# A reordered unit in an attention kernel: where the maximum products, the value products and two VectorE steps stand

## The chip, the core and the metric

One core of a Trainium2 chip runs the whole program. The metric is the device time of one execution in microseconds (us). Engines are named as the profile names them: PE is TensorE's matmuls and PEld its weight loads, DVE is VectorE, ACT is ScalarE, POOL is GpSimd, SP is SyncE, which here only issues DMAs.

## The reference, cut to what matters

The kernel computes a transformer block on x of shape (2, 2048, 256): attention with 16 heads of width 16, a layer norm, a small gated feed-forward part, and a second layer norm.

```
q, k, v = x @ Wq + bq, x @ Wk + bk, x @ Wv + bv      # split into 16 heads of 16
q, k    = q*cos + rot(q)*sin, k*cos + rot(k)*sin     # rotary, interleaved pairs
probs   = softmax(q @ k^T / sqrt(16))                # 2048 x 2048 for each of 2*16 heads
x1      = layernorm(x + (probs @ v))
xr, xk  = mu*x1 + (1 - mu)*previous_token(x1)        # one mu for r, one for k
x2      = sigmoid(xr @ Wr^T) * (relu(xk @ Wk^T)^2 @ Wv^T)
out     = layernorm(x1 + x2)
```

## The kernel before, in words

There are 32 heads (2 sequences x 16), and nearly all of the time is in `period(h)`, once for each. The scores of a head are 2048 x 2048. They are made twice. First, while the head before is at work, PE makes them only to find the maximum of each query row (the **maximum product**, L511, into `ring_ps`), and DVE reduces them (L1095). Then, in the head's own period, they are made again in transposed form with the negated maximum added as three more rows of the contraction (the **score**, L608, into `score_ps`), ACT takes the exponential (L783, into `probs`), and PE multiplies by the values (the **values**, L544, `pv`, into `pv_ps`). Queries and keys are each split into three bf16 parts, so a score has 96 or 99 rows of contraction; the value product is in fp32 and passes twice.

A period has 16 **units** (`kt`). One unit of PE holds

- four scores S0 to S3 of 128 x 512, each as four matmuls of 32 columns of weights side by side (one group of four);
- two maximum products m0 and m1 of the next head, 128 x 1024 each, so two groups of four each. The first is for the first half of the keys of a query tile, the second for the other;
- the values of the unit before, `pv(kt - 1)`, four matmuls in two passes.

In the kernel before they are issued in the order S0, half of m0, S1, half of m0, S2, half of m1, S3, half of m1, `pv`. Two generators make the order: `ring_ops` yields after each half of a maximum product, and the loop over j takes one half after each score.

What binds the engines to each other:

- `ring_ps` has two buffers of 1024 columns. m(k) may start when DVE has reduced m(k-2) (`ring_freed`).
- `score_ps` has three banks. Score n may start when exponential n-3 is done (`exps_done`). `probs` has two buffers of one unit, so ACT's unit kt waits for `pv(kt - 2)` (`pv_done`).
- `period_ops(h)` lists what DVE does in each unit, in order: the two reductions; `cut` (L1074, the 16 row maxima of the whole next head, negated) behind the last reduction of that head, which falls in unit 12; `turn` (L1105, a transpose of `pv_ps` once the head before is summed up) in unit 0; `recip` (L1110, 1/sum) in unit 1; and for heads 17 to 24 `stat` in unit 8 (layer norm statistics, L1121 and L1124), for heads 24 to 27 `flip` in units 6 and 10.
- The maxima of head h+1 go from DVE's `cut` to POOL, which splits them into three bf16 parts with four small operations in a row (`cut_maxima`, L890 to L896), and then to PE, which turns them with two small matmuls (**negatives**, L524, waits on `neg_cut`) at the start of unit 14 (`NEG_CYCLE`). ACT copies the result, SP stores it with a DMA, and the next period starts when it has landed. PE takes its instructions in the order in which they are issued, so whatever is behind the negatives waits with them.
- PE waits for `turn` (`pv_turned`) before the first values of a head, in unit 1.
- POOL's loop, one pass for each head: `lay_v` (the values of a later head), `add_context` (context x 1/sum, added to x; waits for `recip`), a quarter of the rotary work of a coming group of four heads (`turn_quad`, `cut_quad_high`, `_mid`, `_low`), and last `cut_maxima`.
- In the last head there are no maximum products; its units already hold S0, S1, S2, `pv`, S3.

Of the kernel before, what the change touches and what calls it, by code (L numbers as in the profile page):

```python
# [21 lines left out]
BLOCKS = SEQ // TOK  # L22
# [3 lines left out]
LAST = ALL_HEADS - 1  # L26
# [27 lines left out]
R_PER_CYCLE = 1  # L54
FLIPS = 4 * 4
POOL_BLOCKS = 2
STAT_HEAD, STAT_CYCLE = HEADS + 1, 8
FLIP_HEAD, FLIP_CYCLES = HEADS + 8, (6, 10)
MIXED_BUFS = 3
# [24 lines left out]
def period_ops(h):  # L84

    for kt in range(TILES):
        ops = []
        for u in (2 * kt + EARLY, 2 * kt + EARLY + 1):
            if u < MAX_UNITS:
                if h + 1 <= LAST:  # L90
                    ops.append(("max", h + 1, u))
                    if u == MAX_UNITS - 1:
                        ops.append(("cut", h + 1, 0))
            elif h + 2 <= LAST:
                ops.append(("max", h + 2, u - MAX_UNITS))
        if 0 < h < LAST and kt < 2:
            ops.append((("turn", "recip")[kt], h - 1, 0))
        if kt == STAT_CYCLE and 0 <= h - STAT_HEAD < POOL_BLOCKS * TPB:
            ops.append(("stat", h - STAT_HEAD, 0))
        flip = (h - FLIP_HEAD) * len(FLIP_CYCLES)  # L100
        if kt in FLIP_CYCLES and 0 <= flip < POOL_BLOCKS * TPB:
            ops.append(("flip", flip + FLIP_CYCLES.index(kt), 0))
        yield ops
# [7 lines left out]
def ring_len(ops):  # L111
    return sum(kind in ("max", "neg") for kind, _, _ in ops)
# [9 lines left out]
def item(h, kt, j):  # L122

    return h * UNITS + kt * BLOCKS + j + h + (kt >= NEG_CYCLE and h < LAST)


def neg_item(h):

    return item(h - 1, NEG_CYCLE, 0) - 1
# [7 lines left out]
def build(nc, x_tok, x_ch, w_qk, b_qk, w_v, b_v, w_rkv, mu, cos_t, sin_t, ident, ident_h, out):  # L137
# [3 lines left out]
    with ExitStack() as ctx:  # L141
        def sb(name, shape, dt=F32):
            return ctx.enter_context(nc.sbuf_tensor(name, shape, dt))
# [34 lines left out]
        recip = sb("recip", [P, CTX_BUFS, TILES])  # L178
# [157 lines left out]
        def _(sp):  # L336
# [83 lines left out]
            def land(n):  # L420

                sp.wait_ge(flip_ready, (n + 1) * TPB)
                after(sp, edge_ready, n if n > 1 else 0)
                src = flipped_y[:, n % 2, :].rearrange("p (m b t) -> p b m t", m=CHUNKS * TPB, t=VCOLS)
                dst = y_ch[:, n % 2].rearrange("p c (q a t) -> p a (c q) t", q=TPB, t=VCOLS)
                for a in range(P // VCOLS):
                    for b in range(P // VCOLS):
                        sp.dma_start(dst[b * VCOLS:(b + 1) * VCOLS, a], src[a * VCOLS:(a + 1) * VCOLS, b])\  # L428
                            .then_inc(y_landed[n], DMA)

            for h in range(LAST):
# [9 lines left out]
                block, odd = divmod((h + 1 - FLIP_HEAD) * len(FLIP_CYCLES), TPB)  # L441
                if not odd and 1 <= block <= POOL_BLOCKS:
                    land(block - 1)
            for n in range(POOL_BLOCKS, BLOCKS):
                land(n)
# [16 lines left out]
        def _(pe):  # L462
# [55 lines left out]
            def negatives(h, bank):  # L518

                pe.wait_ge(neg_cut, h + 1)  # L520
                rows = neg_cuts[:, :, :].rearrange("p a t -> p (a t)")
                for g in range(0, PARTS * TILES, VCOLS):
                    top = min(g + VCOLS, PARTS * TILES)
                    mm = pe.matmul(bank[g:top, 0:P], rows[:, g:top], id16[:, :], start=True, stop=True)  # L524
                return mm

            def ring_ops(ops, k):

                for kind, h, unit in ops:
                    if kind == "max":  # L530
                        yield from maximum(k, h, unit)
                        k += 1
                    elif kind == "neg":
                        pe.wait_ge(ring_freed, k + 1)
                        negatives(h, ring_ps[k % 2]).then_inc(ring_filled, 1)
                        k += 1
                        yield
# [40 lines left out]
            def beside(kt):  # L578

                if kt == 1:  # L580
                    pe.wait_ge(ring_freed, RING_CREDIT + RING_TOTAL)
                if kt > 0:
                    for _ in itertools.islice(first_r, R_PER_CYCLE):
                        pass
# [4 lines left out]
            def period(h):  # L589

                k = RING_BASE[h]

                pe.wait_ge(neg_in[h % STACKS], (h // STACKS + 1) * DMA)
                for kt, ops in enumerate(period_ops(h)):

                    work = ring_ops(ops, k)
                    k += ring_len(ops)
                    if kt == NEG_CYCLE and h < LAST:
                        n = neg_item(h + 1)
                        pe.wait_ge(exps_done, n + 1)  # L600
                        negatives(h + 1, score_ps[n % SCORE_BANKS]).then_inc(scores_ready, 1)
                    for j in range(BLOCKS):
                        n = item(h, kt, j)
                        queries = q_stack[0:ROWS_M, h % STACKS, :].rearrange("r (c j t) -> r j c t", j=BLOCKS, t=VCOLS)

                        pe.wait_ge(exps_done, n + 1)
                        for g in range(0, P, VCOLS):
                            mm = pe.matmul(score_ps[n % SCORE_BANKS][g:g + VCOLS, :],  # L608
                                           k_stack[0:ROWS_M, h % STACKS, kt * P + g:kt * P + g + VCOLS],
                                           queries[:, j],  # L610
                                           start=True, stop=True)
                        mm.then_inc(scores_ready, 1)
                        next(work, None)
                        if h == LAST and j == BLOCKS - 2:
                            pv_before(h, kt)
                    for _ in work:
                        pass
                    if h < LAST:
                        pv_before(h, kt)
                    else:  # L620
                        beside(kt)
                if h == LAST:
                    for _ in first_r:
                        pass

            def pv_before(h, kt):

                if kt > 0:
                    if kt == 1:
                        pe.wait_ge(v_aug_ready, h + 1)  # L630
                        after(pe, pv_turned, h)
                    pv(h, kt - 1)
                elif h > 0:
                    pv(h - 1, TILES - 1)
# [232 lines left out]
        def _(pool):  # L867
# [31 lines left out]
            def add_context(h):  # L899

                pool.wait_ge(recip_ready, h + 1)
                after(pool, z_ready, h)
                pool.tensor_tensor(ctx_part[:, :, :], ctx_turn[:, h % CTX_BUFS, :, 0:HEAD_DIM],  # L903
                                   recip[:, h % CTX_BUFS].unsqueeze(2).broadcast_to([P, TILES, HEAD_DIM]), ALU.mult)\
                    .then_inc(ctx_ready, 1)
                pool.wait_ge(ctx_ready, h + 1)
                z = z_heads[:, :, h, :]
                pool.tensor_tensor(z, z, ctx_part[:, :, :], ALU.add).then_inc(z_ready, 1)
# [26 lines left out]
            def cut_quad_low(g):  # L935

                pool.wait_ge(quad_step, g * QUAD_STEPS)
                pool.tensor_tensor(cuts[:, g % 2, 2, :], raw, cuts[:, g % 2, 1, :], ALU.subtract).then_inc(quad_ready, 1)  # L938
# [35 lines left out]

            for h in range(ALL_HEADS - 2):
                lay_v(h + 2)
                add_context(h)
                g = 2 + h // QUAD
                if g < QUADS:
                    if h % QUAD == 0:  # L980
                        turn_quad(g)
                    if h % QUAD == 1:
                        cut_quad_high(g)
                    if h % QUAD == 2:
                        cut_quad_mid(g)
                    if h % QUAD == 3:
                        cut_quad_low(g)
                for n in range(POOL_BLOCKS):
                    if h == STAT_HEAD + (n + 1) * TPB - 1:
                        inverse(rstd, n * TPB, (n + 1) * TPB, (n + 1) * TPB, rstd_ready)  # L990
                        normalise(n)
                cut_maxima(h + 2)


            add_context(LAST - 1)
            for n in range(POOL_BLOCKS, BLOCKS):
                inverse(rstd, n * TPB, (n + 1) * TPB, (n + 1) * TPB, rstd_ready)
# [331 lines left out]
```

## Time and profile before

| | |
|---|---|
| median of 3 runs | 1533.99 us (1533.17 to 1534.14) |
| the profiled execution | 1533.71 us, its span 1531.9 us |
| granted TensorE clock, mean | 0.999 |
| PE busy | 1515.3 us, 99% |
| DVE busy | 1339.2 us, 87% |
| ACT busy | 1147.2 us, 75% |
| POOL busy | 335.0 us, 22% |
| DMA | 69.35 MB, mean 45 GB/s |

Busy times are those of the records. Matmuls overlap each other in them, and a reduction or an exponential starts a little before the one ahead of it has ended, so the start of one to the start of the next tells more than the mean duration.

### The profile page before, as it was taken

The page shows a single profiled execution, that of the slowest core. Times are in us where ns is not written, and L with a number is a line of the kernel's source. Part 1 is how long each engine was busy: PE and PEld are TensorE (multiplying, and loading weights), DVE is VectorE, ACT ScalarE, POOL GpSimd, SP SyncE. Part 2 cuts the span into 40 slices and gives each one's busy share as a digit, 9 for nine tenths or more (in the row PEclk, how much of TensorE's full clock was granted, in tenths as well). Part 3 has the DMA queues.
Part 4 walks back from the last instruction along what each step waited for, and adds up shares of the span by engine and source line. Part 5 has one row for each costly group of instructions (what it writes and reads, how often), then busy time and mean ns, then how long its engine had stood idle before and what let it go on. Part 6 is the DMA issues. An engine that isn't in the chain of part 4 may idle for free.

```text
span 1531.9 us, 49389 instructions
## 1 busy us (share of the span) xinstructions
PE 1515.3 (99%) x22016; PEld 728.9 (48%) x22016; DVE 1339.2 (87%) x1413; ACT 1147.2 (75%) x2212; POOL 335.0 (22%) x346
## 2 busy tenths in 40 slices
PE   8999999999999999999999999999999999999998
PEld 3344444444444445444444444454444444443476
DVE  5568999999999999999999999999999999998586
ACT  3338777787787787877877878778777787778855
POOL 2510322132211222132213221042212000000145
PEclk9999999999999999999999999999999999999999
DMA  7724111121112110121112111200111212000102
GB/s 231 239 92 143 29 23 23 23 78 23 23 23 78 23 18 10 22 76 23 23 23 78 23 23 23 75 15 13 23 23 23 37 23 37 2 3 2 29 29 83
DMA packets 48389, 69.35 MB, mean 45 GB/s; under 512 B 23920, under 2 KB 33904, under 8 KB 46384
## 3 DMA queue, kind: packets, MB, share of 16 engines
q1 hardware_dynamic: 45936, 62.81, 17.7%
q8 instruction: 173, 2.83, 0.8%
q10 hardware_dynamic: 2240, 3.38, 0.6%
q14 instruction: 40, 0.33, 0.1%
HBM read 26.97 MB, written 11.53 MB: 25 GB/s over the span
## 4 chain that ended last, share of the span: by engine, by line
PE 93%; DVE 2%; SPq 1%; DMA 1%; POOL 1%; ACT 1%; issue 1%; POOLq 0%; ACTq 0%
PE ring_ps L511 29%; PE score_ps L608 28%; PE pv_ps L544 28%; PE score_ps L488 2%; SPq L428 1%; PE ring_ps L570 1%; PE pv_ps L488 1%; PE score_ps L498 1%; PE score_ps L682 1%; DMA xz<-x_ch 1%; DVE tile_max L1095 0%; PE score_ps L666 0%; PE ring_ps L498 0%; PE pv_ps L666 0%; DVE stats L1121 0%
## 5 line engine op out<-in xcount | busy, mean ns | idle before, releaser
L1095 DVE TENSOR_REDUCE tile_max<-ring_ps 128x1 f32<-128x1024 f32 x1024 | 1204.3, 1216 | 138.5 <-PE ring_ps L511 136.6
L783 ACT ACTIVATE probs<-score_ps 128x512 f32<-128x512 f32 x2048 | 1057.6, 602 | 257.9 <-PE score_ps L608 255.8
L608 PE MATMUL score_ps<-q_stack,k_stack 99*32 99x512 bf16 x8192 | 830.6, 380 | 1.3 <-ACT probs L783 0.9
L511 PE MATMUL ring_ps<-k_stack,q_stack 96*32 96x512 bf16 x8192 | 828.6, 380 | 0.5 <-DVE tile_max L1095 0.4
L544 PE MATMUL pv_ps<-probs,v_aug 128*32 128x512 f32 x4096 | 538.5, 592 | 0.0
L608 PEld LDWEIGHTS score_ps<-q_stack,k_stack 99*32 99x32 bf16 x8192 | 250.7, 95 | 313.9 <-ACT probs L783 146.5
L511 PEld LDWEIGHTS ring_ps<-k_stack,q_stack 96*32 96x32 bf16 x8192 | 249.3, 96 | 302.0 <-DVE tile_max L1095 109.8
L544 PEld LDWEIGHTS pv_ps<-probs,v_aug 128*32 128x32 f32 x4096 | 142.3, 111 | 86.4
L890 POOL TENSOR_TENSOR neg_cuts<-neg_max,zeros 128x16 bf16<-128x16 f32 x32 | 7.1, 222 | 711.0 <-DVE neg_max L1074 711.0
L883 POOL TENSOR_TENSOR v_aug<-v_all,b_v_s 128x256 f32<-128x256 f32 x32 | 23.4, 732 | 278.3 <-PE pv_ps L544 255.9
L488 PE MATMUL score_ps<-xz,w_qk_s 128*32 128x512 f32 x384 | 47.7, 618 | 5.5 <-DMA w_qk_s<-w_qk 4.4
L903 POOL TENSOR_TENSOR ctx_part<-ctx_turn,recip 128x256 f32<-128x256 f32 x32 | 20.0, 624 | 123.7 <-DVE recip L1110 123.7
L743 ACT ACTIVATE probs<-score_ps,b_qk_s 128x512 f32<-128x512 f32 x21 | 14.4, 688 | 30.5 <-PE score_ps L488 30.5
L913 POOL TENSOR_TENSOR rope<-rope 128x2048 f32<-128x2048 f32 x7 | 32.1, 4580 | 22.1 <-DMA rope<-qk_raw 22.1
L570 PE MATMUL ring_ps<-w_rkv_s,rope 128*32 128x256 f32 (+1 forms) x224 | 31.3, 379 | 1.4 <-ACT q_stack L814 1.4
L914 POOL TENSOR_TENSOR rope<-rope 128x2048 f32<-128x2048 f32 x7 | 32.1, 4581 | 0.0
L920 POOL TENSOR_TENSOR rope<-rope 128x2048 f32<-128x2048 f32 x7 | 32.0, 4571 | 0.1
L1173 DVE SCALAR_TENSOR_TENSOR rope<-rope,mu_s 128x512 f32<-128x512 f32 x32 | 21.9, 747 | 9.1 <-ACT rope L808 8.9
L931 POOL TENSOR_TENSOR rope<-rope 128x2048 f32<-128x2048 f32 x7 | 28.8, 4114 | 0.1
L938 POOL TENSOR_TENSOR rope<-rope 128x2048 bf16<-128x2048 f32 x7 | 28.8, 4111 | 0.1
L827 ACT ACTIVATE v_all<-score_ps 128x512 f32<-128x512 f32 x14 | 7.6, 597 | 25.8 <-PE score_ps L682 25.8
L570 PEld LDWEIGHTS ring_ps<-w_rkv_s,rope 128*32 128x32 f32 (+1 forms) x224 | 21.7, 144 | 10.3 <-issue 6.4
(99 smaller groups left out, 529.7 us busy)
## 6 DMA issues: line engine op xcount, KB each, us to landing
qk_raw<-probs SPq DMA_DIRECT2D x28, 256.0 KB, 4.0
rope<-qk_raw SPq DMA_DIRECT2D x7, 1024.0 KB, 4.8
rope<-qk_raw SPq DMA_DIRECT2D x14, 512.0 KB, 6.8
q_stack<-rope SPq DMA_DIRECT2D x31, 192.0 KB, 3.6
k_stack<-rope SPq DMA_DIRECT2D x31, 192.0 KB, 4.2
xz<-x_tok SPq DMA_DIRECT2D x2, 2048.0 KB, 12.5
q_stack<-rope SPq DMA_DIRECT2D x31, 128.0 KB, 3.7
k_stack<-rope SPq DMA_DIRECT2D x31, 128.0 KB, 3.7
```

The lines of the kernel that those rows point to most:

```text
L488: mm = pe.matmul(bank[r:r + VCOLS, :], w_qk_s[:, c, m + r:m + r + VCOLS], x_s[:, b, c, t:t + TOK], start=c == 0, stop=c == CHUNKS - 1)
L511: mm = pe.matmul(ring_ps[k % 2][g:g + VCOLS, c * TOK:(c + 1) * TOK], q_stack[0:ROWS, buf, qt * P + g:qt * P + g + VCOLS], k_stack[0:ROWS, ...
L544: mm = pe.matmul(pv_ps[j * VCOLS:(j + 1) * VCOLS, :], v_aug[:, h % 2, kt, :], probs[:, kt % 2, j, :], start=kt == 0, stop=kt == TILES - 1, ...
L570: mm = pe.matmul(r_ps[n][g:g + width, q * DIM:(q + 1) * DIM], mixed[:, n % MIXED_BUFS, 0, c, q * P + g:q * P + g + width], w_rkv_s[:, 0, c ...
L608: mm = pe.matmul(score_ps[n % SCORE_BANKS][g:g + VCOLS, :], k_stack[0:ROWS_M, h % STACKS, kt * P + g:kt * P + g + VCOLS], queries[:, j], s ...
L783: act.activation(probs[:, kt % 2, j, :], score_ps[n % SCORE_BANKS][:, :], ACT.Exp, scale=SCALE).then_inc(exps_done, 1)
L913: pool.tensor_tensor(raw, raw, cos_s, ALU.mult).then_inc(quad_step, 1)
L914: pool.tensor_tensor(swapped, swapped, sin_s, ALU.mult).then_inc(quad_step, 1)
L920: pool.tensor_tensor(raw, raw, swapped, ALU.add).then_inc(quad_step, 1)
L931: pool.tensor_tensor(raw, raw, cuts[:, g % 2, 0, :], ALU.subtract).then_inc(quad_step, 1)
L938: pool.tensor_tensor(cuts[:, g % 2, 2, :], raw, cuts[:, g % 2, 1, :], ALU.subtract).then_inc(quad_ready, 1)
L1095: dve.reduce_max(tile_max[:, h % 2, unit // 2, unit % 2:unit % 2 + 1], slot[:, :], AX.X)\
```

## The change

It moves instructions and neither adds nor removes any.

1. PE, heads 0 to 30: a unit is now S0, S1, the whole of m0, S2, `pv(kt - 1)`, S3, the whole of m1. (The last head keeps its order.)
2. DVE: `turn` stands between the two reductions of unit 0 and no longer behind both.
3. DVE: `recip` stands behind the reductions of unit 4 and no longer of unit 1.
4. POOL: `add_context(h)` stands behind the quarter of rotary work and no longer ahead of it.

```diff
+RECIP_CYCLE = 4
@@ period_ops
-        if 0 < h < LAST and kt < 2:
-            ops.append((("turn", "recip")[kt], h - 1, 0))
+        if 0 < h < LAST and kt == 0:
+            ops.insert(1, ("turn", h - 1, 0))
+        if 0 < h < LAST and kt == RECIP_CYCLE:
+            ops.append(("recip", h - 1, 0))
@@ tensor engine, period, loop over j
                         mm.then_inc(scores_ready, 1)
-                        next(work, None)
-                        if h == LAST and j == BLOCKS - 2:
+                        if j == 1:
+                            for _ in range(2):
+                                next(work, None)
+                        if j == BLOCKS - 2:
                             pv_before(h, kt)
                     for _ in work:
                         pass
-                    if h < LAST:
-                        pv_before(h, kt)
-                    else:
+                    if h == LAST:
                         beside(kt)
@@ gpsimd, loop over heads
                 lay_v(h + 2)
-                add_context(h)
                 g = 2 + h // QUAD
                 ...
+                add_context(h)
```

PE before, around the negatives (L524), in the order in which it issues. L608 are scores, L511 halves of maximum products, L544 the values; "x4" is one group.

```order
L608 MATMUL score_ps<-q_stack,k_stack 32x512 x4
L511 MATMUL ring_ps<-k_stack,q_stack 32x512 x4
L544 MATMUL pv_ps<-probs,v_aug 32x512 x4
L524 MATMUL score_ps<-id,neg_cuts 32x128
L524 MATMUL score_ps<-id,neg_cuts 16x128
L608 MATMUL score_ps<-q_stack,k_stack 32x512 x4
L511 MATMUL ring_ps<-k_stack,q_stack 32x512 x4
```

The values were the last thing in a unit and stood just ahead of the negatives. The same place now; the lines of the file are three further down (L611, L514, L547, L527).

```order
L611 MATMUL score_ps<-q_stack,k_stack 32x512 x8
L514 MATMUL ring_ps<-k_stack,q_stack 32x512 x8
L611 MATMUL score_ps<-q_stack,k_stack 32x512 x4
L547 MATMUL pv_ps<-probs,v_aug 32x512 x4
L611 MATMUL score_ps<-q_stack,k_stack 32x512 x4
L514 MATMUL ring_ps<-k_stack,q_stack 32x512 x8
L527 MATMUL score_ps<-id,neg_cuts 32x128
L527 MATMUL score_ps<-id,neg_cuts 16x128
L611 MATMUL score_ps<-q_stack,k_stack 32x512 x8
L514 MATMUL ring_ps<-k_stack,q_stack 32x512 x8
```

The second maximum product is now the last thing in a unit, and the values stand between the third score and the fourth.

DVE before, from one head's cut (L1074) to the next's: L1095 are the reductions, L1105 is `turn`, L1110 `recip`.

```order
L1074 TENSOR_REDUCE neg_max<-tile_max 128x16
L1095 TENSOR_REDUCE tile_max<-ring_ps 128x1 x8
L1105 STREAM_TRANSPOSE ctx_turn<-pv_ps 128x512
L1095 TENSOR_REDUCE tile_max<-ring_ps 128x1 x2
L1110 RECIPROCAL recip<-ctx_turn 128x16
L1095 TENSOR_REDUCE tile_max<-ring_ps 128x1 x22
L1074 TENSOR_REDUCE neg_max<-tile_max 128x16
```

And now, for the same stretch:

```order
L1077 TENSOR_REDUCE neg_max<-tile_max 128x16
L1098 TENSOR_REDUCE tile_max<-ring_ps 128x1 x7
L1108 STREAM_TRANSPOSE ctx_turn<-pv_ps 128x512
L1098 TENSOR_REDUCE tile_max<-ring_ps 128x1 x9
L1113 RECIPROCAL recip<-ctx_turn 128x16
L1098 TENSOR_REDUCE tile_max<-ring_ps 128x1 x16
L1077 TENSOR_REDUCE neg_max<-tile_max 128x16
```

The transpose is one reduction earlier, the reciprocal six later, and the cut still follows the 32nd reduction of a head.

## Rows read from the trace of the kernel before

**Rows 1.** The page, part 1: busy time and share of each engine.
```profile
PE 1515.3 (99%) x22016; PEld 728.9 (48%) x22016; DVE 1339.2 (87%) x1413; ACT 1147.2 (75%) x2212; POOL 335.0 (22%) x346
```

**Rows 2.** The page, part 5: busy, mean ns of one, idle before it and releaser.
```profile
L1095 DVE TENSOR_REDUCE tile_max<-ring_ps 128x1 f32<-128x1024 f32 x1024 | 1204.3, 1216 | 138.5 <-PE ring_ps L511 136.6
L608 PE MATMUL score_ps<-q_stack,k_stack 99*32 99x512 bf16 x8192 | 830.6, 380 | 1.3 <-ACT probs L783 0.9
L511 PE MATMUL ring_ps<-k_stack,q_stack 96*32 96x512 bf16 x8192 | 828.6, 380 | 0.5 <-DVE tile_max L1095 0.4
```

**Rows 3.** The waits: who waited for whom, us in total, times, longest.
```profile
PEld score_ps L608 <- ACT probs L783: 146.5, 619, 0.8
PEld ring_ps L511 <- DVE tile_max L1095: 109.8, 335, 0.6
```

**Rows 4.** Timeline, head 8, PE: start us, length, what, merged.
```profile
448.37 1.09 PE L544 MATMUL pv_ps<-probs,v_aug 128*32 128x512 f32 x8
...
450.44 0.40 PE L511 MATMUL ring_ps<-k_stack,q_stack 96*32 96x512 bf16 x4
...
451.10 1.03 PE L544 MATMUL pv_ps<-probs,v_aug 128*32 128x512 f32 x8
...
464.13 1.03 PE L544 MATMUL pv_ps<-probs,v_aug 128*32 128x512 f32 x8
...
476.98 0.39 PE L511 MATMUL ring_ps<-k_stack,q_stack 96*32 96x512 bf16 x4
477.19 1.04 PE L544 MATMUL pv_ps<-probs,v_aug 128*32 128x512 f32 x8
...
479.80 1.04 PE L544 MATMUL pv_ps<-probs,v_aug 128*32 128x512 f32 x8
...
480.68 0.22 PE L524 MATMUL score_ps<-id,neg_cuts 128*16 128x128 bf16 x2
...
480.88 0.45 PE L511 MATMUL ring_ps<-k_stack,q_stack 96*32 96x512 bf16 x4
```

**Rows 5.** Timeline, head 8, DVE; in brackets the idle time before.
```profile
445.17 2.36 DVE L1095 TENSOR_REDUCE tile_max<-ring_ps 128x1 f32<-128x1024 f32 x2 [0.25 <-PE ring_ps L511]
447.44 0.71 DVE L1105 STREAM_TRANSPOSE ctx_turn<-pv_ps 128x512 f32<-128x512 f32 x1
448.07 2.32 DVE L1095 TENSOR_REDUCE tile_max<-ring_ps 128x1 f32<-128x1024 f32 x2
450.31 0.23 DVE L1110 RECIPROCAL recip<-ctx_turn 128x16 f32<-128x16 f32 x1
...
453.06 2.36 DVE L1095 TENSOR_REDUCE tile_max<-ring_ps 128x1 f32<-128x1024 f32 x2 [0.31 <-PE ring_ps L511]
...
476.55 2.36 DVE L1095 TENSOR_REDUCE tile_max<-ring_ps 128x1 f32<-128x1024 f32 x2 [0.26 <-PE ring_ps L511]
478.94 0.19 DVE L1074 TENSOR_REDUCE neg_max<-tile_max 128x16 f32<-128x32 f32 x1
```

**Rows 6.** Timeline, head 8, POOL, units 12 and 13.
```profile
479.21 0.22 POOL L890 TENSOR_TENSOR neg_cuts<-neg_max,zeros 128x16 bf16<-128x16 f32 x1 [23.08 <-DVE neg_max L1074]
...
480.11 0.22 POOL L896 TENSOR_TENSOR neg_cuts<-neg_rest,neg_cuts 128x16 bf16<-128x16 f32 x1
```

**Rows 7.** Timeline, head 8, PE's weight loads ahead of unit 14.
```profile
480.44 0.12 PEld L524 LDWEIGHTS score_ps<-id,neg_cuts 128*32 128x32 bf16 x2 [0.51 <-ACT probs L783]
```

**Rows 8.** Timeline, head 17, DVE, unit 8.
```profile
845.55 0.42 DVE L1121 BATCH_NORM_STATS2 stats<-xz 128x6 f32<-128x256 f32 x1
...
846.10 4.77 DVE L1095 TENSOR_REDUCE tile_max<-ring_ps 128x1 f32<-128x1024 f32 x4
```

**Rows 9.** Timeline, head 8, ACT, unit 13.
```profile
478.57 2.07 ACT L783 ACTIVATE probs<-score_ps 128x512 f32<-128x512 f32 x4 [0.55 <-PE score_ps L608]
```

**Rows 10.** Timeline, the opening, PE: a whole maximum product, then fp32 projections.
```profile
76.68 0.62 PE L511 MATMUL ring_ps<-k_stack,q_stack 96*32 96x512 bf16 x8
77.12 1.90 PE L488 MATMUL score_ps<-xz,w_qk_s 128*32 128x512 f32 x16
```

## The prediction

> **What bounds the kernel now.** I read the page's busy times first: PE 99% of the span, DVE 87%, ACT 75%, POOL 22% [rows 1]. Then the groups by line: scores and maximum products have almost no PE idle time ahead of them (1.3 and 0.5 us in all) [rows 2]. Then the waits: weight loads wait 146.5 us for exponentials and 109.8 us for reductions [rows 3], but a load stands ahead of its matmul, so most of that is hidden. Last the timeline of one ordinary head, number 8, to see what a unit costs and where it is longer.
>
> From the values of unit 1 to those of unit 6 PE takes (464.13 - 451.10) / 5 = 2.606 us a unit [rows 4]. One group of four has 0.218 us, the values the rest, 2.606 - 8 x 0.218 = 0.86. That is PE streaming without a gap, and the change leaves its amount alone. Units 6 to 11 take (477.19 - 464.13) / 5 = 2.612. One unit a head is much longer: 451.10 - 448.37 = 2.73 [rows 4]. So all that any order can win is the excess over 2.606: 0.12 a head there, and 0.006 in each later unit. What it can lose is any wait that becomes longer than the lead of PE's loads.
>
> Times below are within a unit, in us, with 0 at the first score. New places on PE: S0 0, S1 0.22, m0 0.44 and 0.65, S2 0.87, values 1.09 to 1.95, S3 1.95, m1 2.17 and 2.39, end 2.606. Before: m0 0.22 and 0.65, m1 1.09 and 1.53, values 1.74.
>
> **Durations used.** From the start of a maximum product's last group to its reduction, where DVE was idle: that group of unit 2 begins at 451.10 + 0.86 + 3 x 0.218 = 452.61, the reduction at 453.06, so 0.45 [rows 4, 5]. From one reduction to the next (447.44 - 445.17) / 2 = 1.135; a reduction lasts 1.216 [rows 2, 5]. From its end to the matmul that waited for its buffer: 448.07 + 2.32 = 450.39 to 450.44, 0.05 [rows 4, 5].
>
> **The excess at the head's start goes.** Before, the transpose (448.07 - 447.44 = 0.63 until the next reduction) stood behind both reductions of unit 0, so those of unit 1 were late, and m1 of unit 2 had to wait: the load that began at 450.44 [rows 4, 5]. Now m0 of unit 0 is reduced from 1.37 (behind m1 of the unit before, filled at 2.39 + 0.45 = 0.23 of this one). The transpose follows at 2.50; the values it needs are done at 1.09 + 1.09 = 2.18. The reduction of m1, ready at 2.84, starts at 3.13 and frees its buffer at 4.40, wanted at 4.78. That of m0 in unit 1 starts at 4.27 and frees at 5.54, wanted at 5.65. No wait is left, with 0.11 to spare. Gain 0.124 x 30 heads = 3.7 us; bounds 0 (the 0.11 is used up) and 3.7. PE waits for the transpose ahead of the values of unit 1, at 3.70; it ends at 3.21.
>
> **The negatives become late.** This is the term that decides. The chain is: last reduction of a head in unit 12, cut, four POOL operations, PE's load for the negatives, due at the start of unit 14. Head 8: the second reduction of the pair at 476.55 starts at 476.55 + 1.135 = 477.69, the cut at 478.94, POOL at 479.21, its last operation ends at 480.11 + 0.22 = 480.33, and PE's load begins 0.11 later, at 480.44 [rows 5, 6, 7]. So 2.75 from reduction to load. The matmul runs at 480.68 [rows 4]: the load, which had waited for POOL, came only 0.24 ahead of it. There is no more slack than that.
> Before, the product was filled at 476.98 + 0.45 = 477.43 and its reduction queued 0.26 behind that of m0. Now m1 is the last thing in unit 12: its last group begins 2.606 + 0.218 = 2.82 ahead of unit 14, is filled 2.37 ahead of it, and DVE is idle then (m0's reduction makes room at 2.50, m1 comes at 2.84). The load comes 2.75 - 2.37 = 0.38 behind the place where PE could have started the negatives. With 0.02 from load to matmul and the loads of the next score, 0.40 of standstill. Everything is queued behind the negatives on PE: S0 of unit 14 and all that follows. 30 heads x 0.40 = +12.0 us. Lower bound 0.28 (the weight load's own 0.12 [rows 7] turns out to be hidden): 8.4. Upper bound 0.38 + 0.12 + 0.12 for loads not hidden: 0.62, 18.6. I take 0.40, since the wait at 450.44 shows a matmul starting right behind what freed it.
> Head 30 apart: no maximum products follow unit 12, so PE is not full there. The standstill is 0.4 too, but the values of unit 11 (0.86) are already done when m1 ends. I take -0.5, bounds -1 and +1.
>
> **The exponentials.** The fourth one used to be far ahead of need and is not now. The first starts 0.52 behind S0 (478.57 against 477.19 + 0.86 = 478.05), and four take 2.07 [rows 4, 9]. S3 at 1.95 is taken up at 2.47 and done at 3.07 + 0.05, which is 0.52 in the next unit. S2 (0.87) and the values (1.09) need it: hidden, 0.35 spare. In unit 14 the negatives take one of the three score banks, and there S1 needs it, at 0.22. That would be a standstill of 0.30 of its own; it is covered by the 0.40 ahead of it, and is the price if the chain through POOL were quicker than I think.
>
> **Statistics, heads 17 to 24.** 846.10 - 845.55 = 0.55 on DVE behind m1 of unit 8 [rows 8]. The next m0 is then reduced from 2.84 + 1.135 + 0.55 = 4.52 and frees at 5.79, wanted at 5.65: 0.14 x 8 = +1.1 us. Before, it delayed m0 by little, since that was queued anyway. The flips (heads 24 to 27) stand at the same place; I count 0 for them, at most the same 1.1.
>
> **Reciprocal and context.** In unit 4 the reciprocal (0.23 [rows 5]) shifts m0's reduction to 4.20 at most, freed at 5.47, wanted at 5.65: hidden. Who waits for it is POOL's context, which now stands behind at most two rotary operations; POOL is busy 22% [rows 1] and had waited 23.08 us idle for the cut in head 8 [rows 6]. Nothing on PE waits for the context before the tail. 0.
>
> **The small excess.** S3's loads have more lead now (the second exponential is under way by 1.2, so the first is done, and S3 is at 1.95), and m1's too. Of 0.006 x 10 units x 30 heads = 1.8 us I take half, -0.9; bounds -1.8 and, since the cause is not visible, +1.8.
>
> **Sum.** 12.0 + 1.1 - 3.7 - 0.5 - 0.9 = +8.0 on the profiled execution's 1533.7 (span 1531.9, 1.8 outside it): 1541.7. The median of the runs shown is 0.3 higher; I leave the forecast at 1541.7.
>
> **Rivals.**
> A. The order wins and nothing is late. It needs a chain from reduction to load shorter by 0.4, and the fourth exponential earlier too. Then 1533.7 - 3.7 - 0.9 - 0.5 + 1.1 = 1529.7. For it: the excess at the head's start is plain in the timeline. Against it: the load for the negatives already waited for POOL, and the move of m1 is arithmetic of PE's order. The point from which it decides: both below 0.05 a head.
> B. The chain is partly hidden and the fourth exponential binds, 0.30 x 30 = 9.0: 1533.7 + 9.0 + 1.1 - 5.1 = 1538.7.
> C. The standstill is longer than the arithmetic, 0.6: S1 also waits, or loads are exposed. 18.0 + 1.1 - 5.1 = +14.0: 1547.7.
> D. Two groups of one kind in a row stream faster than alternating ones, so a unit's floor falls. The opening has whole maximum products in a row: 77.12 - 76.68 = 0.44 for two groups, 0.22 each [rows 10], not less than 0.218. If three pairs a unit saved 0.005 each, 496 units would give 7.4 and the time would be 1534.3, no change.
> The Trainium skill bears on D: "TensorE: Matmul & The Clock Gate", section Back-to-back issue gap, gives a gap of N / 2.4 ns plus about 2.5, which is 216 ns for 512 columns; if the eight groups of a unit fell to that from 0.218, the estimate by that page is 0.016 a unit, 8 us in all. The trace has no run of bf16 groups at that gap.
>
> **Chances.** Forecast 0.64, B 0.12, C 0.13, A 0.07, D 0.04. A measurement tells 0.2% (3.1 us) from no change. Slower: forecast, B and C, less a little for B's lower end, 0.87. Same: D and that end, 0.06. Faster: A, 0.07. The range runs from B's lower half to most of the way to C: 1537.0 to 1546.0.
>
> **What would show it.** Right: PE idle ahead of the negatives' line, about 0.4 x 31, put down to POOL; the load for them right behind POOL's last operation; the unit after a head's first values back at 2.61; a longer unit behind the statistics in heads 17 to 24; the reduction of unit 12's m1 starting some 2.4 ahead of unit 14 and not 3.0. Wrong: heads no longer than before (16 x 2.606 + 0.12 + 0.06 = 41.9 us), or standstills that fall in every unit.

## The result: 0.36% slower, by a late chain that gives up more than the order wins

| | median | against before, 95% interval |
|---|---|---|
| before, measured again beside it | 1533.84 us (6 runs) | |
| changed | 1539.55 us (1539.03 to 1540.32, 6 runs) | 1.0036 [1.0026, 1.0046] |
| forecast | 1541.7, range 1537.0 to 1546.0 | 1.0051 |

All times here and below are medians of fast runs; one slow run of the kernel before, 3252.78 us beside e1 to e4, is left out.

The profiled execution has a span of 1537.2 us, 5.3 more than before. Part 1 of its page, to be held against [rows 1]:

```profile
PE 1512.5 (98%) x22016; PEld 768.9 (50%) x22016; DVE 1344.2 (87%) x1413; ACT 1199.9 (78%) x2212; POOL 335.0 (22%) x346
```

PE's busy time fell by 2.8 us while the program became longer: PE now stands still somewhere. Yet the waits of its weight loads, to be held against [rows 3], are nearly gone for scores and maximum products. PE itself now has idle time ahead of the negatives (who waited for whom: us in all, times, longest):

```profile
PEld score_ps L611 <- ACT probs L786: 18.4, 53, 0.6
PEld score_ps L527 <- ACT probs L786: 15.5, 20, 2.0
PEld ring_ps L514 <- DVE tile_max L1098: 12.2, 48, 0.5
PE score_ps L527 <- ACT probs L786: 7.2, 30, 0.3
PE score_ps L527 <- POOL neg_cuts L899: 1.4, 1, 1.4
```

109.8 us of waiting for reductions became 12.2, and 146.5 for exponentials 18.4. (The idle time of the same loads that is put down to issue, where nothing in the profile holds them, rose from 66.2 and 54.2 to 164.2 and 138.6.) None of that was worth much: PE had had only 1.3 and 0.5 us of idle time there [rows 2]. What counts are the last two lines, PE's own idle time ahead of the negatives: 8.6 us in 31 heads, where the kernel before had 0.3 us, once. Even that is only a part, as the next rows show. (The loads for the negatives, L527, don't show it as clearly: they had waited 16.4 us before, and now 15.5 put down to ACT and 7.7 put down to issue.) The same head as in [rows 4, 5], PE's timeline at the start of unit 14 (start us, length, what):

```profile
480.39 1.06 PE L547 MATMUL pv_ps<-probs,v_aug 128*32 128x512 f32 x8
481.25 0.41 PE L611 MATMUL score_ps<-q_stack,k_stack 99*32 99x512 bf16 x4
481.47 0.63 PE L514 MATMUL ring_ps<-k_stack,q_stack 96*32 96x512 bf16 x8
482.33 0.23 PE L527 MATMUL score_ps<-id,neg_cuts 128*32 128x128 bf16 x2 [0.24 <-ACT probs L786]
```

Two groups from 481.47 end their turn at 481.47 + 0.43 = 481.90, and the negatives run at 482.33: 0.43 of standstill. The bracket shows only 0.24 of it, since the records of the matmuls before it run on, and names ACT. Its exponentials say otherwise:

```profile
479.12 2.29 ACT L786 ACTIVATE probs<-score_ps 128x512 f32<-128x512 f32 x4 [0.31 <-PE score_ps L611]
481.72 0.60 ACT L786 ACTIVATE probs<-score_ps 128x512 f32<-128x512 f32 x1 [0.31 <-PE score_ps L611]
```

The negatives take the bank of three scores back, the second of unit 13, and its exponential is the third of the four that end at 481.41. The one behind them, for the fourth score, ends at 482.32, when the load for the negatives has already begun (482.30), so nothing of ACT held it. DVE, POOL and PE's loads show who did:

```profile
479.56 1.22 DVE L1098 TENSOR_REDUCE tile_max<-ring_ps 128x1 f32<-128x1024 f32 x1 [0.24 <-PE ring_ps L514]
480.81 0.19 DVE L1077 TENSOR_REDUCE neg_max<-tile_max 128x16 f32<-128x32 f32 x1
```

```profile
481.08 0.22 POOL L893 TENSOR_TENSOR neg_cuts<-neg_max,zeros 128x16 bf16<-128x16 f32 x1 [19.41 <-DVE neg_max L1077]
...
481.97 0.22 POOL L899 TENSOR_TENSOR neg_cuts<-neg_rest,neg_cuts 128x16 bf16<-128x16 f32 x1
```

```profile
482.30 0.12 PEld L527 LDWEIGHTS score_ps<-id,neg_cuts 128*32 128x32 bf16 x2 [0.70 <-issue]
```

POOL ends at 482.19 and the load begins 0.11 later, the same step as in [rows 6, 7]; the whole chain takes 482.30 - 479.56 = 2.74, as before. Only its start has moved: 2.34 ahead of the negatives' due time (481.90) and no longer 2.97 (477.69 to 479.80 + 0.86 = 480.66).

The head's start went as forecast. DVE there, to be held against [rows 5]:

```profile
445.78 2.36 DVE L1098 TENSOR_REDUCE tile_max<-ring_ps 128x1 f32<-128x1024 f32 x2 [0.24 <-PE ring_ps L514]
448.05 0.71 DVE L1108 STREAM_TRANSPOSE ctx_turn<-pv_ps 128x512 f32<-128x512 f32 x1
448.68 4.65 DVE L1098 TENSOR_REDUCE tile_max<-ring_ps 128x1 f32<-128x1024 f32 x4
```

The transpose now takes up idle time that DVE had between the reductions of two units, and four reductions follow without a gap until DVE has caught up. PE's unit 2 is as short as its neighbours.

From the starts of the values in every unit of heads 0 to 29, summed by kind, changed less before:

| | before, a unit | after, a unit | units | sum, us | forecast |
|---|---|---|---|---|---|
| unit 2 of a head | 2.734 | 2.602 | 29 | -3.8 | -3.7 |
| the unit with the negatives | 2.617 | 3.054 | 30 | +13.1 | +12.0 |
| behind the statistics | 2.618 | 2.776 | 8 | +1.3 | +1.1 |
| all others | 2.612 | 2.599 | 413 | -5.1 | -0.9 |
| head 30 and after, net of the first start | | | | +0.3 | -0.5 |

That is +5.8 at the last values, and +5.7 in the medians. In the last row, the starts from head 30 on give +1.0, but the very first values of the program start 0.7 earlier. The values stand 0.65 earlier in a unit now, and in the last head they don't, so 0.7 of the +1.0 is that shift of place and no time lost.

### The profile page after: what moved, and what is told of

It reads as the page before. It is cut to its first block, busy times and chain, and to the rows that moved or that the text cites. A ratio compares the mean times of both kernels' runs of the same rounds, so it can differ in the third digit from the quotient of the medians.

```text
span 1537.2 us, 49389 instructions
## 1 busy us (share of the span) xinstructions
PE 1512.5 (98%) x22016; PEld 768.9 (50%) x22016; DVE 1344.2 (87%) x1413; ACT 1199.9 (78%) x2212; POOL 335.0 (22%) x346
## 4 chain that ended last, share of the span: by engine, by line
PE 92%; DVE 2%; ACT 2%; SPq 1%; DMA 1%; POOL 1%; issue 1%; POOLq 0%; ACTq 0%
PE score_ps L611 28%; PE ring_ps L514 28%; PE pv_ps L547 28%; PE score_ps L491 2%; ACT probs L786 1%; SPq L431 1%; PE ring_ps L573 1%; PE pv_ps L491 1%; PE score_ps L501 1%; PE score_ps L685 1%; DMA xz<-x_ch 1%; PE score_ps L527 0%; PE pv_ps L669 0%; PE ring_ps L501 0%; PE score_ps L669 0%
## 5 line engine op out<-in xcount | busy, mean ns | idle before, releaser
L786 ACT ACTIVATE probs<-score_ps 128x512 f32<-128x512 f32 x2048 | 1110.2, 598 | 211.2 <-PE score_ps L611 155.5
L611 PE MATMUL score_ps<-q_stack,k_stack 99*32 99x512 bf16 x8192 | 744.2, 380 | 1.0 <-ACT probs L786 0.7
L514 PE MATMUL ring_ps<-k_stack,q_stack 96*32 96x512 bf16 x8192 | 645.0, 379 | 0.2 <-DVE tile_max L1098 0.2
L547 PE MATMUL pv_ps<-probs,v_aug 128*32 128x512 f32 x4096 | 540.8, 592 | 0.0
L514 PEld LDWEIGHTS ring_ps<-k_stack,q_stack 96*32 96x32 bf16 x8192 | 265.7, 97 | 297.6 <-issue 164.2
L611 PEld LDWEIGHTS score_ps<-q_stack,k_stack 99*32 99x32 bf16 x8192 | 260.8, 95 | 283.6 <-issue 138.6
L547 PEld LDWEIGHTS pv_ps<-probs,v_aug 128*32 128x32 f32 x4096 | 148.1, 111 | 80.0
```

The lines of the kernel that those rows point to most:

```text
L514: mm = pe.matmul(ring_ps[k % 2][g:g + VCOLS, c * TOK:(c + 1) * TOK], q_stack[0:ROWS, buf, qt * P + g:qt * P + g + VCOLS], k_stack[0:ROWS, ...
L547: mm = pe.matmul(pv_ps[j * VCOLS:(j + 1) * VCOLS, :], v_aug[:, h % 2, kt, :], probs[:, kt % 2, j, :], start=kt == 0, stop=kt == TILES - 1, ...
L611: mm = pe.matmul(score_ps[n % SCORE_BANKS][g:g + VCOLS, :], k_stack[0:ROWS_M, h % STACKS, kt * P + g:kt * P + g + VCOLS], queries[:, j], s ...
L786: act.activation(probs[:, kt % 2, j, :], score_ps[n % SCORE_BANKS][:, :], ACT.Exp, scale=SCALE).then_inc(exps_done, 1)
```

## The experiments

Each was timed with the kernel before beside it on the same chip: e1 to e4 on one chip (before 1534.06), e5 to e7 on a second (1534.38), e8 and e9 on a third (1534.30). Ratios are to that one, with 95% intervals. Where a time is compared in us with the changed kernel's 1539.55, that was taken in another sitting, and half a microsecond can't be told.

**e1, the maxima a unit earlier.** The cut then falls in unit 11, and the negatives stay.

```diff
-EARLY = 2 * LEAD
+EARLY = 2 * LEAD + 2
```

> The changed kernel, with every maximum product one unit earlier (EARLY 8 instead of 6), so the cut falls in unit 11 and the negatives, still at the start of unit 14, find their chain done 2.6 us earlier. The theory (PE stands still for 0.446 us a head because the chain reduction, cut, four POOL operations ends late, 12.9 us over 29 heads): that wait goes. By its second part the score S1 of unit 14 then waits for the fourth exponential of unit 13, 0.30 a head by the prediction's arithmetic, so only 0.15 x 30 = 4.4 us come back: 1535. Rival 1, that the chain was all of it and the exponential is in time: 0.446 x 30 = 13.4 us come back, 1526. Rival 2, that the standstill has another cause (the turn of the negatives itself, the score bank): no change, 1539.5, and PE's load for the negatives still waits.

Measured: 1532.72 us, 0.9989 of before [0.998, 0.9999]. The unit with the negatives is 2.839, 0.24 over the others, where it had been 0.45. POOL, PE and PE's loads there:

```profile
437.62 0.22 POOL L899 TENSOR_TENSOR neg_cuts<-neg_rest,neg_cuts 128x16 bf16<-128x16 f32 x1
```

```profile
439.74 0.61 PE L514 MATMUL ring_ps<-k_stack,q_stack 96*32 96x512 bf16 x8
440.17 0.23 PE L527 MATMUL score_ps<-id,neg_cuts 128*16 128x128 bf16 x2
```

```profile
439.96 0.10 PEld L527 LDWEIGHTS score_ps<-id,neg_cuts 128*16 128x16 bf16 x2
439.97 0.31 PEld L611 LDWEIGHTS score_ps<-q_stack,k_stack 99*32 99x32 bf16 x4
440.61 0.10 PEld L611 LDWEIGHTS score_ps<-q_stack,k_stack 99*32 99x32 bf16 x4 [0.34 <-ACT probs L786]
```

```profile
439.96 0.60 ACT L786 ACTIVATE probs<-score_ps 128x512 f32<-128x512 f32 x1 [0.31 <-PE score_ps L611]
```

POOL is done 2.3 us ahead, and the negatives follow the maximum product 0.43 after its start, without a gap. The standstill is one score later, at the load of S1 at 440.61, and this time ACT is the right name: the fourth exponential ends at 439.96 + 0.60 = 440.56, 0.05 ahead of that load. Both rivals fail: the time is neither 1526 nor 1539.5, and the load for the negatives no longer waits. The second wait had been hidden behind the first, at 0.24 a head and not the 0.30 of the arithmetic. The gain of 6.8 us over the changed kernel is more than the 4.4 expected.

**e2, the same with the negatives in unit 13, between the values and S3.**

```diff
-NEG_CYCLE = TILES - LEAD + 1
+NEG_CYCLE = TILES - LEAD
 def item(h, kt, j):
-    return ... + (kt >= NEG_CYCLE and h < LAST)
+    return ... + ((kt, j) >= (NEG_CYCLE, BLOCKS - 1) and h < LAST)
 # PE and ACT: negatives and copy_neg ahead of j == BLOCKS - 1
```

> As e1, and the negatives stand in unit 13 between the values and S3 instead of at the start of unit 14; ACT copies them between its third and fourth exponential. The chain ends 0.4 us into unit 13, the negatives are issued at 1.95, and S3 behind them needs only the second exponential (done at 1.7). The theory: no standstill of either kind, 13.4 us less than the changed kernel: 1526, some 8 us below the kernel before. Rival: an order of this kind has a standstill wherever the negatives take a bank, then it is at the level of e1 (1535).

Measured: 1528.29 us, 0.9962 [0.9947, 0.9977]. The unit with the negatives is 2.606 on average, 0.006 over an ordinary one, so both waits are gone. It is 2 us short of the forecast: an ordinary unit is 2.600 and not 2.597, and unit 2 has 0.04 again (0.06 in e6). Why unit 2 has it wasn't settled.

**e3, PE's order alone.** Transpose, reciprocal and context where they were before.

```diff
-RECIP_CYCLE = 4
+RECIP_CYCLE = 1
-            ops.insert(1, ("turn", h - 1, 0))
+            ops.append(("turn", h - 1, 0))
 # and add_context(h) ahead of the rotary work again
```

> The changed kernel with PE's new order alone: the transpose behind both reductions of unit 0, the reciprocal in unit 1, and POOL's context ahead of the rotary work, as before the change. The theory: m1 is ready at 2.84 in a unit now, so the transpose starts at 3.97 and ends at 4.68, while the values of unit 1 want it at 3.70: PE stands still about 1.0 us a head, 30 us in all: 1570. Rival: the transpose's place only moves the wait for the ring (0.22 a head): 1546. If the move of the transpose was worth only the 3.7 us that the excess had cost before: 1543.

Measured: 1572.87 us, 1.0251 [1.0236, 1.0266]. DVE and PE in units 0 and 1 of head 8:

```profile
457.12 0.70 DVE L1108 STREAM_TRANSPOSE ctx_turn<-pv_ps 128x512 f32<-128x512 f32 x1
```

```profile
454.20 1.07 PE L547 MATMUL pv_ps<-probs,v_aug 128*32 128x512 f32 x8
...
457.93 0.64 PE L547 MATMUL pv_ps<-probs,v_aug 128*32 128x512 f32 x4 [0.92 <-issue]
```

The values of unit 1 start 0.11 behind the transpose's end (457.82), 3.73 after the last ones and not 2.60: 1.13 a head. e8 below has the reciprocal and the context in their old places too, but the transpose in its new one, and takes 1539.07. So it is the transpose's place that counts, and in the new order it is worth not 3.7 us but 33.

**e4, the first maximum product in alternating halves again.**

```diff
-                        if j == 1:
-                            for _ in range(2):
-                                next(work, None)
+                        if j < 2:
+                            next(work, None)
```

> The changed kernel with the first maximum product in halves between the scores again (S0, half, S1, half, S2, values, S3, m1 whole). Tests where the shorter unit comes from (2.597 us in the changed kernel, 2.606 to 2.612 before). Theory: a change of kind behind two groups of one kind costs 215 ns from start to start and any other step 219; this order has one such step a unit (m1 to S0) instead of three, so 2.605 in an undisturbed unit, 0.008 x 496 = 4 us more. On top, m0 wants its buffer at 0.22 instead of 0.44: by the arithmetic 0.1 a head in unit 2 and 0.36 in the eight statistics heads, 6 us. Sum: 1549. Rival: the shorter unit comes from the values' new place and the longer lead of the loads, then the undisturbed unit stays at 2.597 here and the time is about 1545.

Measured: 1548.24 us, 1.009 [1.0074, 1.0107]. The median unit is 2.605 against 2.599, near the theory of the step. Of the 8.7 us over the changed kernel that is only some 2.5. The rest is m0 waiting for its buffer: unit 2 has 2.712 (3.2 us in all), the units behind the statistics 2.956 (1.4), and those behind the flips 2.761 (1.3, which nobody had forecast; in the changed kernel the flips cost nothing, 2.597). The starts of the groups, medians in ns from one to the next over some 460 units, beginning with the values' two passes:

```
before   V 432 V 428 S 219 m 218 S 219 m 219 S 219 m 219 S 219 m 219 V   2611
changed  V 432 V 428 S 219 m 219 m 215 S 219 S 215 m 219 m 215 S 219 V   2600
e4       V 432 V 428 S 219 m 218 m 215 S 219 m 218 S 219 m 218 S 219 V   2605
e5       V 432 V 428 S 218 S 215 m 219 m 215 S 224 S 227 m 220 m 215 V   2613
e9       V 432 V 428 S 219 S 215 m 219 m 215 S 219 m 219 S 219 m 219 V   2604
```

It is not the second of a pair that comes sooner. It is what stands behind the pair, 215 and not 219. "A change of kind behind a pair" says too much, though: the opening of the kernel before has one place with four groups of maximum products in a row, and they start 220, 215 and 215 ns apart, with the next kind 216 behind the last. In the timeline:

```profile
96.09 1.05 PE L511 MATMUL ring_ps<-k_stack,q_stack 96*32 96x512 bf16 x16
96.95 1.92 PE L498 MATMUL pv_ps<-w_v_s,xz 128*32 128x256 f32 x32
```

Those four groups take 0.866 in all. So the plainer reading is that each change of kind costs about 4 ns, once, from the start of the first group of the new kind to the next start: nine changes in a unit before, six now, eight in e4, seven in e9, five in e5. The values fit (432 for their first pass, 428 for the second). Groups of one kind in a row also use the same columns of weights here, so kind and weights aren't told apart.

**e5, all in pairs.** As e2, with the values behind the second score.

```diff
-                        if j == BLOCKS - 2:
+                        if j == (BLOCKS - 3 if h < LAST else BLOCKS - 2):
                             pv_before(h, kt)
```

> As e2 (maxima a unit earlier, negatives in unit 13 behind the values), with the values between the second score and the third: S0, S1, m0 whole, values, S2, S3, m1 whole, so that scores come in pairs too. Theory of the step (215 ns for a change of kind behind two groups of one kind, 219 else): four such steps a unit instead of three, 2.596 instead of 2.600, 2 us less in all. But the values now want the fourth exponential of the unit before at 0.87, and by the durations it is done at 0.81 at the earliest, as the fourth score comes when the third is still waited for: at best hidden, else up to 0.1 a unit. So between 1526 (step theory, all hidden) and 1575 (0.1 in every unit). Rival: the step depends on something else and the unit is 2.600 with the wait apart.

Measured: 1535.36 us, 1.0007 [0.9998, 1.0016]. The row above has three of the four steps of 215; the fourth, from the second score to the maximum product, is 227, and the one ahead of it 224. In these two PE waits a few ns. Loads of scores now wait for ACT 1476 times, 478.7 us in all, where the changed kernel had 53 such waits. In one unit of the timeline the exponential that started at 460.98 ends at 461.58, and the load for the second score, which takes its bank, begins at 461.63. So it is the second score that waits, for the exponential three scores back, and not the values for the fourth, as the expectation had it. A unit is 2.613, 17 ns over the 2.596 of the theory, while the order was to win 4.

**e6, the statistics between the reductions too.** As e2, and

```diff
-            ops.append(("stat", h - STAT_HEAD, 0))
+            ops.insert(1, ("stat", h - STAT_HEAD, 0))
```

> As e2, with the layer norm statistics of heads 17 to 24 between the two reductions of unit 8 instead of behind both. Theory: DVE is idle for about 0.34 us there in every unit, so of the 0.21 a head by which unit 9 was longer in e2 nothing is left: 8 x 0.21 = 1.7 us less than e2 (1528.3), 1526.6. Rival: the statistics cost the same wherever they stand, 1528.3.

Measured: 1526.78 us (1526.57 to 1526.94), 0.9951 [0.9939, 0.9964]. The eight units behind the statistics have 2.601 on average, after 2.808 in e2. The times alone hardly part e6 from e2 (the intervals overlap); these units do. It is the fastest version found, 7.6 us below the kernel before and 12.8 below the changed one.

**e7, the chain made longer.** The changed kernel with one more POOL operation ahead of the last.

```diff
+                pool.tensor_tensor(neg_spare[:, :], neg_rest[:, :], zeros[:, :], ALU.add).then_inc(neg_step, 1)
```

> The changed kernel with one more small POOL operation (a copy of the rest into a spare tile, nobody reads it) inside the chain from the cut to the negatives; from start to start such an operation takes 0.30 us. Theory: the chain sets the standstill ahead of the negatives, so all of it is paid in every head, 30 x 0.30 = 9 us more than the changed kernel: 1548.5. Rival, that the standstill is the exponential's or the score bank's: no change, 1539.5.

Measured: 1549.71 us, 1.0101 [1.0087, 1.0114], 10.2 more than the changed kernel. PE, head 8:

```profile
441.89 0.66 PE L515 MATMUL ring_ps<-k_stack,q_stack 96*32 96x512 bf16 x8
443.08 0.23 PE L528 MATMUL score_ps<-id,neg_cuts 128*32 128x128 bf16 x2 [0.54 <-POOL neg_cuts L902]
```

The unit with the negatives is 0.315 longer for an operation of 0.30, so all of the chain is on the path. The matmul's bracket now names POOL, in all 31 heads; that of its load still names ACT in 30.

**e8, reciprocal and context back.** The transpose stays.

```diff
-RECIP_CYCLE = 4
+RECIP_CYCLE = 1
 # and add_context(h) ahead of the rotary work again
```

> The changed kernel with two of its parts undone: the reciprocal in unit 1 again and POOL's context ahead of the rotary work again; the transpose stays between the reductions. Theory: both are beside PE's path, 1539.5 within 1 us. Rival: in unit 1 DVE is still behind from the transpose, so the reciprocal there delays m0 of unit 2 past its 0.1 of spare: up to 0.15 x 30 = 4 us more, 1544.

Measured: 1539.07 us, 1.0033 [1.0022, 1.0043]. The two parts have no effect that can be told; unit 2 has 0.005 over 2.597, as in the changed kernel.

**e9, one pair in the kernel before.**

```diff
-                        next(work, None)
+                        if j > 0:
+                            for _ in range(2 if j == 1 else 1):
+                                next(work, None)
```

> The kernel before with one thing changed: the first maximum product whole behind the second score (S0, S1, m0 whole, S2, half of m1, S3, half of m1, values). The values, DVE's steps and the place of the last maximum product's reduction stay. Theory of the step: two changes of kind stand behind a pair of one kind (S1 to m0, m0 to S2), each 4 ns shorter, so a unit is 0.008 shorter: 496 x 0.008 = 4 us less than before, 1530. Rival, that the shorter unit of the changed kernel comes from the values' place or the longer lead of the loads: no change from 1534, or slower, since S0 and S1 come 0.2 closer together.

Measured: 1530.59 us, 0.9977 [0.9968, 0.9987], 3.7 below the kernel before. PE in head 8, from one unit's values to the next's:

```profile
463.35 1.04 PE L544 MATMUL pv_ps<-probs,v_aug 128*32 128x512 f32 x8
464.21 0.62 PE L608 MATMUL score_ps<-q_stack,k_stack 99*32 99x512 bf16 x8
464.64 0.61 PE L511 MATMUL ring_ps<-k_stack,q_stack 96*32 96x512 bf16 x8
465.07 0.40 PE L608 MATMUL score_ps<-q_stack,k_stack 99*32 99x512 bf16 x4
```

Two scores and the whole product take 0.43 each, and a unit 2.604. With the values, the transpose and the last reduction in their old places the two pairs alone give 7 of the forecast 8 ns, so neither the values' place nor the loads' lead is needed for it.

## Why the prediction was right, point by point

- **The head's start.** Right to 0.1 us in sum. The transpose, due at 2.50 in its unit, was there, and no reduction after it was late. What the prediction didn't ask was what PE's order costs without that move; e3 gives 33 us.
- **The negatives.** Right in mechanism, place and size: +13.1 against +12.0. The start of the chain is at 2.34 ahead of the due time (2.37 worked out), its length is 2.74 (2.75), and 0.44 a head is lost against 0.40. e1 takes the chain away and e7 lengthens it, and the time follows each. A mark named for it was wrong: the profile puts PE's wait down to ACT in 30 heads and to POOL in one.
- **The exponential behind it.** The prediction said that a second wait of 0.30 lay under the first. e1 laid it bare at 0.24.
- **Statistics.** 0.16 x 8 = 1.3 against 1.1; e6 moves it into DVE's gap and it is gone. The flips, counted at 0, cost nothing.
- **Reciprocal and context.** Costed at nothing, and e8 shows it.
- **The small excess: the term mis-sized.** The step read: "Of 0.006 x 10 units x 30 heads = 1.8 us I take half, -0.9". Measured, -5.1. It took 2.606 for the floor of a unit. The changed order has a lower floor, 2.597 to 2.600, by three steps of 215 in place of 219 ns. Rival D had named such a thing with a chance of 0.04, at 7.4 us, and dismissed it by [rows 10]: two groups of one kind, 0.44 from the first to what stands behind them, "0.22 each". That 0.44 is 220 + 215 ns, so the shorter step was in the row, and rounding to 0.22 hid it. The prediction also says that the trace has no run of bf16 groups at 216 ns; the row at 96.09, shown under e4, is one.
- **What the sum owes to luck.** The forecast was 2.2 us too high, and that is less than this one error. The floor gave 4.2 us more than forecast, and the other terms came out 2.0 us dearer (the negatives 1.1, head 30 0.8, the statistics 0.2, the head's start -0.1).
- **Head 30.** +0.3 against -0.5, within its bounds, but not for the reason given. The standstill there was to grow by 0.4. It grew by 1.09: from 0.44 (PE free at 1402.68, negatives at 1403.12) to 1.53 (1407.38 to 1408.91). PE has no maximum products behind unit 12 and reaches the negatives sooner, and the chain took 3.02 there and not 2.74. The rest, from head 30 on, gave 0.8 of that back.

The time alone doesn't choose between the forecast and rival B: 1539.55 is nearer to B's 1538.7 than to 1541.7. The trace and two runs choose. PE stands still ahead of the negatives and S0, not ahead of S1, 0.44 a head and not 0.30 (against B) or 0.6 (against C); e7 adds to it all of what the chain got longer; and B's wait for the exponential appears, at 0.24, only when e1 has taken the chain away.

## What to carry to other kernels

Before moving the last producer of a chain that ends in a full engine, add up the chain from that producer to the consumer and compare it with the lead of the consumer's weight load, not with the idle time that the profile shows: 0.24 us of lead was all there was here. When a wait is taken away, compute the one that lies under it, and move both: e1 alone won 7 us, e2 and e6 another 6. And where the profile names an engine as the cause of a wait, check that one's last instruction against the load's start before believing it.

## What the runs showed of the hardware

- From the start of a group of scores or maximum products to the next start are 218 to 220 ns when the group ahead of it was of another kind, and 215 when it was of its own kind. It held in all five orders of the table and in the opening. e4, e5 and e9 were forecast from it in its narrower form, a change of kind behind a pair; in e5 one of the four short steps was lost to a wait. Why isn't shown: the kinds differ in rows (96 and 99), in the tiles that they read, in their weights and in their banks, and none was varied alone.
- From the end of a POOL operation to the weight load that waited for it are 0.11 us, in head 8 of the kernel before, of the changed one and of e7 (442.94 to 443.05):

```profile
442.72 0.22 POOL L902 TENSOR_TENSOR neg_cuts<-neg_rest,neg_cuts 128x16 bf16<-128x16 f32 x1
```

```profile
443.05 0.12 PEld L528 LDWEIGHTS score_ps<-id,neg_cuts 128*32 128x32 bf16 x2 [1.00 <-ACT probs L787]
```

- A POOL operation on 16 columns takes 0.22, but in a chain where each waits for the last they start 0.30 apart (479.21 to 480.11 for three steps in [rows 6]), and one more of them costs a head 0.315 (e7).
